# A fused attention and ternary-weight FFN block on eight cores: vector and scalar work of an attention tile spread otherwise over its four steps, weight scales in two steps, another order where the two phases meet

## The chip, the cores and the metric

The kernel runs on the 8 cores of one Trainium2 chip. Each core works on its own two sequences and no data passes between cores. The metric is the device time of the slowest core, in microseconds (us).

## The reference, cut to what matters

```python
x = L0_attn_x                      # (16, 2048, 1024) float32
x = x + attention(layernorm(x), w_qkv, w_out)   # 16 heads of 64, causal, window of 128 keys
x = x + ffn(layernorm(x), W1, b1, W2, b2)       # 1024 -> 4096 -> 1024
# attention: q, k, v = x @ w_qkv; softmax(q k^T / 8, masked) @ v; @ w_out
# ffn: h = gelu(bitlinear(x, W1, b1)); bitlinear(h, W2, b2)
def bitlinear(x, W, b):
    w_scale = clip(mean(abs(W)), 1e-5)           # one number for the whole matrix
    Wq = clip(round(W / w_scale), -1, 1) * w_scale
    x_scale = clip(max(abs(x), axis=-1), 1e-5)   # one number for each token
    xq = clip(round(x * 127 / x_scale), -128, 127) * x_scale / 127
    return xq @ Wq.T + b
```

## The kernel before, in words

A core has 32 tiles of 128 tokens. The program is written as lists of instructions for each engine (`QUEUE`), in the order in which the Python code calls the helpers; every engine runs its list in order and waits on semaphores (`tok`) for what it needs. So the place of a call in the code is the place in the queue of its engine, and for DMAs in the queue of SyncE (`sp`) or GpSimd (`pool`).

**Phase one** is attention. Its loop runs over 128 steps `j`, four (`c` = 0 to 3) for each tile `t`; step `c` treats four of the 16 heads. In step `j` TensorE gets: the scores of step `j + 1` (`s_pe`, tile `sc`), a first group of other matmuls (`f1`), the product of probabilities and values for step `j - 1` (`av_pe`, tile `av`), the transposes of the probabilities of step `j` (`t_pe`, tiles `tA`, `tB`), and a second group (`f2`). The groups come from `fill`: for c = 0 the queries and for c = 1 the keys of tile `t + 1` (`qk_pe`, 32 matmuls of 128 columns each), for c = 2 the output projection of tile `t - 1` (`o_pe`, 8 matmuls of 512 columns each), for c = 3 the values of tile `t + 1` (`v_pe`). Both groups go to the two banks `fb`, tile `f`. Their evictions (`e1`, and `e2`, which runs in the next step as `prev_ev`) are on ScalarE, but those of c = 2 are the residual adds on VectorE (`resid`, L238, `xr<-f,xr`); the second of them runs in step c = 3 and frees the bank for that step's `f2`.

In each step VectorE adds the mask to the four score tiles and takes their extremes (`ttr`, L455, `msc<-sc,masks`), ScalarE exponentiates (`ex`, `probs<-msc`), VectorE copies the transposed probabilities from PSUM (`pt_ev`, `PT<-tA`). `norm` divides by the sums (c = 2 for the first half of the heads, c = 0 of the next tile for the second), and `at_tr` transposes the result by DMA (`attnT<-attn`).

The layernorm ahead of attention goes by `ln1_stats` (VectorE, `lnc<-xr`), `ln1_rstd` (ScalarE), `ln1_nmr` (VectorE, one small operation, L339), `xln_` (GpSimd, `xln<-xr,lnc`) and `x_tr` (DMA transpose by SyncE, `xlnT<-xln`). Here the statistics of tile `t + 3` are in step c = 3, and the other four for tile `t + 2` at the end of step c = 0. The layernorm ahead of the FFN needs `ln2_sum` (mean, VectorE) and `ln2_sq` (sum of squares, ScalarE, `junk<-xr,nmean`); `spill` writes the tile to HBM by GpSimd's queue (`x1sp<-xr`). All three are at the end of step c = 0, two tiles later. `load_x` waits for the spill of the tile that had its buffer.

Besides, the FFN's weights are made ready in 128 **tasks**, one or two a step from step 4 on (`at_step`). `a1`, `a2` add up the absolute values of a piece of W1, W2 (even pieces on VectorE, odd ones on ScalarE); `q1`, `q2` quantize a piece: `task_pool` scales it on GpSimd one step ahead (`tern<-stg,wsc`), then VectorE clips it (`tern<-tern`) and writes fp8 (L668, `W1q<-tern`, `W2q<-tern`). Each piece is loaded by SyncE's queue (`task_load`, 512 KB, `stg<-w1t`, `stg<-w2t`). `scale_pe` makes the scale of a matrix: VectorE adds the sums, a matmul with ones adds over the partitions, VectorE divides.

**Phase two** is the FFN, a loop over 32 token tiles `it`: 8 groups of up projections of tile `it + 1` (`w1_pe`, banks `sc` and `f`), each evicted by `pre_gelu` (VectorE, `hb`), `gelu` (ScalarE), and `hmax`; then `fh`, `rnd` (ScalarE), `unoff` (VectorE) quantize, `tq` transposes by DMA (`hqT<-hq`), and `w2_pe` does the 64 down projections of tile `it` (`av<-W2q,hqT`). The input of a tile is read back by `load_x1`, `front_pool` subtracts the mean, `front_dve` takes the maximum and rounds, and `xt` transposes (`xlnT<-xln`). Where the phases meet, tiles 30 and 31 of phase one already carry `front_dve` for the first token tiles and up projections of token tile 0. The biases are loaded over the place of the qkv weights, once the last value matmul has read them.

Of the kernel before, what the change touches and what calls it, by code (L numbers as in the profile page):

```python
# [42 lines left out]
def _build(nt):  # L43
# [18 lines left out]
    def sb(name, n, dt, at=None):  # L62
# [3 lines left out]
        if at is None:  # L66
# [46 lines left out]
            for i in range(2, 6)]  # L113
    tern = [sb("tern%d" % i, D, BF16) for i in range(2)]
# [22 lines left out]
    yb = msc  # L137
    xqb = xln
    hqb = hq.bitcast(BF16)

    with ExitStack() as ctx:
# [452 lines left out]
        for i in range(32):  # L594
            tasks.append(("q1", i))
            tasks.append(("a2", i))
# [86 lines left out]

        def load_bias(i):
            if i < 4:
                tk["b1", i] = dma("sp", b1b[:, i * D:(i + 1) * D],
                                  b1_d[i * D:(i + 1) * D].partition_broadcast(
                                      128), d_bias[i], [tok("V", nt - 1, 1)])
            else:
                tk["b2"] = dma("sp", b2b, b2_d.partition_broadcast(128),  # L690
                               d_bias[4], [tok("V", nt - 1, 1)])

# [11 lines left out]
        def front_dve(t):  # L704
# [7 lines left out]
                   ALU.mult, ALU.mult, [r])  # L712
            tk["dq", t] = ts("dve", c[:, 4:5], c[:, 1:2], wsc[:, 3:4], None,
                             ALU.mult, waits=[a, tok("thr", 0)])
            a = ts("dve", xq, xcb[t % 2], c[:, 3:4], RND,
                   ALU.mult, ALU.add,
                   [r, tok("xqT", t - 1) if t else tok("xlnT", nt - 1)])
# [26 lines left out]
        def pre_gelu(t, u):  # L744
# [3 lines left out]
                hb[u % 4], ub[b], c[:, 4:5], b1b[:, u * 512:(u + 1) * 512],  # L748
# [106 lines left out]
        ln1_stats(2)  # L855
# [18 lines left out]
        assert max(j for j in range(nstep) if at_step[j]) <= nstep - 10  # L874
        to_load = list(range(ntask))
# [28 lines left out]
        for j in range(nstep):  # L904
# [14 lines left out]
            for n in mine:  # L919
                if n == 32:  # L920
                    scale_pe(0)
                if n == 96:
                    scale_pe(1)
                if n in (32, 96):
                    task_pool(n)
            for n in at_step[j + 1] if nxt else ():
                if tasks[n][0][0] == "q" and n not in (32, 96):
                    task_pool(n)
# [5 lines left out]
            if prev_ev is not None:  # L934
                prev_ev()
# [208 lines left out]
```

How the kernel before makes its waits and increments, by code:

```python
            def body(eng):  # L1079
                seen = {}
                for waits, fn, s, amt in QUEUE[q]:
                    for ws, val in waits:
                        if val > 0 and seen.get(ws.name, 0) < val:
                            eng.wait_ge(ws.h, val)
                            seen[ws.name] = val
                    if fn is None:
                        continue
                    ins = fn(eng)
                    if s is not None:
                        ins.then_inc(s.h, amt)
```

## Time and profile before

| | us |
|---|---|
| three runs: median (lowest to highest) | 1655.97 (1623.61 to 1711.35) |
| the profiled execution, its own time | 1623.96 |
| its span on the slowest core (core 6) | 1622.4 |
| the other cores' spans | 1607.0 to 1621.3 |
| TensorE busy (matmuls) | 1492.2 (92%) |
| VectorE busy | 1082.6 (67%) |
| ScalarE busy | 785.3 (48%) |
| GpSimd busy | 240.6 (15%) |
| mean granted TensorE clock | 0.985 |

The times are those of the slowest core in one execution. Busy time of an engine is the time in which it has an instruction at work; matmuls overlap, and are counted once. A stretch of the span in which no engine is full is one in which they wait for each other.

### The profile page before, as it was taken

What the parts mean: (1) busy time and instruction counts of PE and PEld (TensorE: products, weight loads), DVE (VectorE), ACT (ScalarE), POOL (GpSimd) and SP (SyncE); (2) the same over time, 40 slices, a digit from 0 to 9 for tenths busy, and PEclk for the clock granted to TensorE, in tenths of its full rate; (3) what the DMA queues carried; (4) which work ended last, traced back from release to release, by engine and by line L of the source; (5) the groups of instructions that cost most, each with busy time, mean ns of one, the idle gap of its engine ahead of it and who ended that gap; (6) DMA issues with size and microseconds to landing.
All of it is one profiled execution on the core that took longest, in us unless ns stands there. A gap on an engine that the chain in (4) does not pass through costs nothing.

```text
span 1622.4 us, 33796 instructions; the slowest of 8 cores (1607.0 to 1622.4 us)
## 1 busy us (share of the span) xinstructions
PE 1492.2 (92%) x11668; PEld 832.4 (51%) x11732; DVE 1082.6 (67%) x2704; ACT 785.3 (48%) x1826; POOL 240.6 (15%) x199
## 2 busy tenths in 40 slices
PE   2798799989999988977999999999999999999998
PEld 2566566666666666633444444444444444444443
DVE  2577788878888888666666666666666666666652
ACT  3677766766676666644433334233333333333331
POOL 0000022112212333102110101010101010110100
PEclk9899999999999999988999999999999999999999
DMA  9977767666655677352525343434435242435232
GB/s 299 266 194 215 210 176 221 190 196 196 212 155 170 180 173 174 84 130 59 111 66 110 66 103 74 97 79 82 94 73 104 66 107 63 111 66 111 65 85 53
DMA packets 277080, 214.25 MB, mean 132 GB/s; under 512 B 239280, under 2 KB 239408, under 8 KB 276912
## 3 DMA queue, kind: packets, MB, share of 16 engines
q1 hardware_dynamic: 272304, 195.31, 48.4%
q0 software_dynamic: 4608, 16.78, 3.0%
q8 instruction: 96, 1.57, 0.4%
q14 instruction: 72, 0.59, 0.1%
HBM read 120.29 MB, written 33.55 MB: 95 GB/s over the span
## 4 chain that ended last, share of the span: by engine, by line
PE 65%; DVE 14%; issue 6%; DMA 6%; ACT 5%; SPq 2%; POOL 1%; DVEq 0%; ACTq 0%; POOLq 0%
PE av L202 28%; PE f L202 23%; PE sc L202 14%; DVE msc L455 5%; DMA xr<-xc 2%; DVE PT L251 2%; ACT junk L218 2%; SPq L188 2%; DMA wst<-wqkv 1%; DVE absc L243 1%; DVE xr L238 1%; ACT probs L218 1%; DVE tern L225 1%; DMA x1sp<-xr 1%; DVE lnc L325 1%
## 5 line engine op out<-in xcount | busy, mean ns | idle before, releaser
L202 PE MATMUL av<-W2q,hqT 128*128 128x512 fp8e4 x2048 | 448.6, 380 | 3.4 <-DMA hqT<-hq 3.4
L218 ACT ACTIVATE hbuf<-hb 128x512 f32<-128x512 f32 x256 | 160.7, 629 | 460.6 <-DVE hb L235 460.5
L202 PEld LDWEIGHTS av<-W2q,hqT 128*128 128x128 bf16 x2048 | 200.9, 98 | 246.0 <-issue 5.7
L218 ACT ACTIVATE probs<-msc,cells 128x256 bf16<-128x256 f32 (+1 forms) x512 | 250.8, 491 | 145.6 <-DVE cells L455 111.9
L202 PE MATMUL f<-xlnT,wqkv_sb 128*128 128x128 bf16 x4096 | 254.6, 221 | 25.6 <-ACT qT L218 23.5
L202 PEld LDWEIGHTS f<-xlnT,wqkv_sb 128*128 128x128 bf16 x4096 | 235.5, 99 | 42.9 <-issue 42.4
L202 PE MATMUL f<-W1q,xlnT 128*128 128x512 fp8e4 x1040 | 238.0, 382 | 5.2 <-DVE hb L235 3.3
L202 PE MATMUL sc<-W1q,xlnT 128*128 128x512 fp8e4 x1008 | 230.2, 382 | 9.2 <-DVE hb L235 9.2
L455 DVE CUSTOM_DVE_ANT_0 msc<-sc,masks 128x256 f32<-128x256 f32 (+1 forms) x512 | 181.8, 410 | 26.5 <-PE sc L202 21.8
L218 ACT ACTIVATE hq<-hbuf,konst,fhc 128x1024 f16<-128x1024 f32 x128 | 148.3, 1229 | 93.4 <-DVE fhc L223 93.4
L202 PEld LDWEIGHTS f<-W1q,xlnT 128*128 128x128 bf16 x1040 | 101.9, 98 | 129.1 <-issue 8.7
L202 PEld LDWEIGHTS sc<-W1q,xlnT 128*128 128x128 bf16 x1008 | 98.9, 98 | 130.1 <-issue 12.8
L235 DVE SCALAR_TENSOR_TENSOR hb<-f,fqc,b1b 128x512 f32<-128x512 f32 x130 | 97.1, 748 | 89.9 <-PE f L202 87.9
L202 PE MATMUL f<-wqkv_sb,xlnT 128*128 128x512 bf16 x480 | 116.9, 386 | 38.9 <-ACT vh L218 17.7
L243 DVE TENSOR_REDUCE fhc<-hbuf 128x1 f32<-128x1024 f32 x128 | 152.0, 1208 | 0.0
L235 DVE SCALAR_TENSOR_TENSOR hb<-sc,fqc,b1b 128x512 f32<-128x512 f32 x126 | 94.2, 748 | 71.4 <-PE sc L202 71.1
L225 POOL TENSOR_SCALAR stg<-xr,nmean 128x1024 f32<-128x1024 f32 x32 | 35.9, 1121 | 697.2 <-DMA xr<-x1sp 552.0
L223 DVE TENSOR_SCALAR hq<-hq 128x1024 bf16<-128x1024 f16 x128 | 58.4, 458 | 110.2 <-ACT hq L218 110.2
L202 PE MATMUL f<-wout_sb,attnT 128*128 128x512 bf16 x465 | 111.0, 380 | 5.8 <-issue 4.9
L225 POOL TENSOR_SCALAR xln<-xr,lnc 128x1024 bf16<-128x1024 f32 x32 | 39.4, 1231 | 405.9 <-ACT qT L218 324.2
L218 ACT ACTIVATION_READ_ACCUMULATOR probs<-msc,cells 128x1 f32 x512 | 96.3, 188 | 0.0
L202 PEld LDWEIGHTS f<-wqkv_sb,xlnT 128*128 128x128 bf16 x512 | 45.8, 98 | 90.7 <-issue 46.0
(78 smaller groups left out, 1356.6 us busy)
## 6 DMA issues: line engine op xcount, KB each, us to landing
stg<-w1t SPq DMA_DIRECT2D x64, 512.0 KB, 7.8
stg<-w2t SPq DMA_DIRECT2D x64, 512.0 KB, 5.8
xr<-xc SPq DMA_DIRECT2D x32, 512.0 KB, 6.0
x1sp<-xr POOLq DMA_DIRECT2D x32, 512.0 KB, 3.4
xr<-x1sp SPq DMA_DIRECT2D x32, 512.0 KB, 5.4
y<-msc SPq DMA_DIRECT2D x32, 512.0 KB, 3.8
wst<-wqkv SPq DMA_DIRECT2D x24, 512.0 KB, 17.6
wst<-wout SPq DMA_DIRECT2D x8, 512.0 KB, 19.4
```

The source lines that it names most:

```text
L188: lambda e: e.dma_start(out=out, in_=in_), s, 16))
L202: return op("pe", lambda e: e.matmul(out=out, lhsT=lhsT, rhs=rhs, start=start, stop=stop), waits, sig)
L218: return op("act", lambda e: e.activation(out=out, in_=in_, func=func, **kw), waits)
L223: return op(q, lambda e: e.tensor_scalar(out=out, in0=in0, scalar1=s1, scalar2=None, op0=op0), waits)
L225: return op(q, lambda e: e.tensor_scalar(out=out, in0=in0, scalar1=s1, scalar2=s2, op0=op0, op1=op1), waits)
L235: return op("dve", lambda e: e.scalar_tensor_tensor(out=out, in0=in0, scalar=s, in1=in1, op0=op0, op1=op1), waits)
L238: return op("dve", lambda e: e.scalar_tensor_tensor(out=out, in0=in0, scalar=s, in1=in1, op0=op0, op1=op1, accum_out=accum), waits)
L243: return op("dve", lambda e: e.tensor_reduce(out=out, in_=in_, axis=AX.X, op=o, apply_absolute_value=absv), waits)
L251: return op("dve", lambda e: e.tensor_copy(out=out, in_=in_), waits)
L325: i=x[:, h * 512:(h + 1) * 512]: e.bn_stats(out=o, in_=i),
L455: e.tensor_tensor_reduce(out=u, in0=i, in1=m, scale=-0.125, scalar=BIG, op0=ALU.add, op1=ALU.min, accum_out=a), w)
```

## The change

The arithmetic is the same. In phase one, `ln1_stats` moves from c = 3 to c = 1, one tile later (for tile `t + 2`); `ln1_rstd` to c = 2, behind the first two exponentials; `ln1_nmr`, `xln_` and `x_tr` to c = 2, behind `norm`. `ln2_sum` and `spill` move to c = 3 of the tile in which the residual is added, and `ln2_sq` to c = 0 behind the first two exponentials. The copy of the probabilities goes to ScalarE at c = 2 when this step has a quantizing task (before: at c = 3, for the later tasks), and at c = 0 and 1 of the last tile.

The task list starts with four more sums of W2, so that quantizing begins later; `scale_pe` is split into `scale_sum`, one step after the last sum, and the matmul, one step after that.

Where the phases meet, the first 1024 biases get a buffer of their own, in the place of `tern`, and are loaded in tile 29 together with the first `load_x1`; `front_dve` is split into `front_max` and `front_q`, which move: those of token tile 0 to c = 1 and 2 of tile 30, those of tile 1 to c = 3 of tile 31, those of tile 2 into the loop of phase two. Four of the eight up projections of token tile 1 come between the last output projection and the loop.

```diff
+    b1q = sb("b1q", D, F32, at=tern_at)
...
         tasks = [("a1", i) for i in range(32)]
-        for i in range(32):
+        tasks += [("a2", i) for i in range(4)]
+        for i in range(28):
             tasks.append(("q1", i))
-            tasks.append(("a2", i))
+            tasks.append(("a2", i + 4))
+        tasks += [("q1", i) for i in range(28, 32)]
...
+        def scale_sum(g):
+            tk["wsum", g] = red(wsc[:, 10 + g:11 + g],
+                                absc[:, 32 * g:32 * g + 32],
+                                ALU.add, [tok("absa", g), tok("absv", g)])
+
         def scale_pe(g):
             b = tbank()
-            v = red(wsc[:, 10 + g:11 + g], absc[:, 32 * g:32 * g + 32],
-                    ALU.add, [tok("absa", g), tok("absv", g)])
             p = mm(tbf[b][:, 0:1], ones, wsc[:, 10 + g:11 + g], True, True,
-                   [v, tfree[b], tok("ones")], sig=True)
+                   [tok("wsum", g), tfree[b], tok("ones")], sig=True)
...
-        ln1_stats(2)
         for hh in range(4):
             ex(0, hh)
...
             if prev_ev is not None:
                 prev_ev()
+            if c == 3 and t >= 1:
+                ln2_sum(t - 1)
+                spill(t - 1)
             if nxt:
                 ex(j + 1, 0)
                 ex(j + 1, 1)
+            if c == 0 and t >= 2:
+                ln2_sq(t - 2)
+            if c == 2 and t + 2 < nt:
+                ln1_rstd(t + 2)
             if f1 is not None:
                 f1()
...
             if c == 2:
                 norm(t, 0)
+                if t + 2 < nt:
+                    ln1_nmr(t + 2)
+                    xln_(t + 2)
+                    x_tr(t + 2)
             t_pe(j)
-            pt_ev(j, on_act=(c == 3 and any(n >= 96 for n in mine)))
+            pt_ev(j, on_act=((c == 2 and any(tasks[n][0][0] == "q"
+                                             for n in mine))
+                             or (late and c < 2)))
...
-            if c == 0:
-                if t >= 2:
-                    ln2_sum(t - 2)
-                    ln2_sq(t - 2)
-                if t + 2 < nt:
-                    ln1_rstd(t + 2)
-                    ln1_nmr(t + 2)
-                    xln_(t + 2)
-                    x_tr(t + 2)
-                if t >= 2:
-                    spill(t - 2)
-            if c == 3 and t + 3 < nt:
-                ln1_stats(t + 3)
+            if c == 1 and t + 2 < nt:
+                ln1_stats(t + 2)
+            if j in sum_step:
+                scale_sum(sum_step[j])
+            if j - 1 in sum_step:
+                scale_pe(sum_step[j - 1])
...
+            if t == nt - 3 and c == 3:
+                load_x1(0)
+                load_bias(0)
             if t == nt - 2:
                 if c == 0:
-                    load_x1(0)
-                if c == 1:
                     ln2_rstd(0, nt - 4)
-                    load_x1(1)
                     front_pool(0, [tok("task", n) for n in
                                    range(ntask - 2, ntask)])
+                if c == 1:
+                    load_x1(1)
+                    front_max(0)
                 if c == 2:
-                    front_dve(0)
+                    front_q(0)
                     front_pool(1)
                 if c == 3:
                     xt(0)
-                    for i in range(5):
+                    for i in range(1, 5):
                         load_bias(i)
             if late:
-                if c == 0:
+                if c == 1:
                     load_x1(2)
-                    front_dve(1)
                 if c == 2:
                     for u in range(4):
                         gelu(0, u)
+                if c == 3:
+                    front_max(1)
+                    front_q(1)
...
-        for h in range(2):
-            o_pe(lt, h, av[:, h * 512:(h + 1) * 512], tok("N", lt, 1))
-            resid(lt, h, av[:, h * 512:(h + 1) * 512])
         hmax(0, 2)
         hmax(0, 3)
         fh(0)
+        for h in range(2):
+            o_pe(lt, h, av[:, h * 512:(h + 1) * 512], tok("N", lt, 1))
         for r in range(4):
             rnd(0, r)
-            unoff(0, r)
+        for u in range(4):
+            w1_pe(1, u)
+            pre_gelu(1, u)
+            unoff(0, u)
+        for r in range(4):
+            tq(0, r)
+        for u in range(4):
+            gelu(1, u)
...
-        front_dve(2)
...
+            if it == 0:
+                front_max(2)
+                front_q(2)
             if it + 2 < nt:
                 xt(it + 2)
```

## Rows read from the trace of the kernel before

**Rows 1.** Windows: length, then busy and (count) of PE, PEld, DVE, ACT, POOL; clock.

```profile
72.17:93.64 21.47, 18.34 (x236) 13.21 (x238) 15.15 (x51) 14.38 (x46) 1.20 (x1) 1.00 1.02 237
...
93.64:673.06 579.42, 520.36 (x6637) 372.66 (x6692) 469.29 (x1557) 399.47 (x1244) 121.23 (x121) 0.99 0.66 184
...
571.57:592.13 20.56, 18.60 (x240) 13.25 (x242) 17.13 (x57) 13.96 (x43) 6.20 (x6) 1.00 0.69 177
...
654.48:673.06 18.58, 18.27 (x239) 13.30 (x240) 11.86 (x48) 13.28 (x42) 2.24 (x3) 1.00 0.29 65
...
687.00:717.79 30.79, 22.15 (x143) 10.03 (x145) 19.92 (x65) 12.48 (x39) 0.70 (x2) 0.83 0.58 137
...
717.79:756.39 38.60, 27.56 (x136) 12.28 (x136) 27.99 (x47) 15.59 (x23) 12.62 (x8) 0.87 0.34 82
...
756.39:770.20 13.81, 13.81 (x65) 6.27 (x64) 8.47 (x19) 5.34 (x6) 0.00 (x0) 1.00 0.11 20
```

**Rows 2.** Timeline of TensorE in tile 25: start, length, instruction, idle before.

```profile
576.25 0.39 PE L202 MATMUL sc<-kT,qT 64*128 64x256 bf16 x4
...
581.26 0.39 PE L202 MATMUL sc<-kT,qT 64*128 64x256 bf16 x4
...
586.06 0.39 PE L202 MATMUL sc<-kT,qT 64*128 64x256 bf16 x4
...
590.52 1.67 PE L202 MATMUL f<-wqkv_sb,xlnT 128*128 128x512 bf16 x7 [1.56 <-ACT vh L218]
```

**Rows 3.** Timeline of the other engines in tile 25; one tile's instructions, ns.

```profile
578.86 0.16 DVE L339 SCALAR_TENSOR_TENSOR lnc<-lnc 128x1 f32<-128x1 f32 x1 [1.92 <-ACT lnc L218]
...
579.38 1.19 POOL L225 TENSOR_SCALAR xln<-xr,lnc 128x1024 bf16<-128x1024 f32 x1 [4.74 <-ACT qT L218]
...
580.71 1.93 SPq L197 DMA_TRANSPOSE xlnT<-xln  x1
...
580.96 1.86 DVE L668 TENSOR_SCALAR W2q<-tern 128x1024 fp8e4<-128x1024 bf16 x1
...
589.47 0.69 DVE L238 SCALAR_TENSOR_TENSOR xr<-f,xr 128x512 f32<-128x512 f32 x1
...
L668 DVE TENSOR_SCALAR W2q<-tern x32: 693/694/1864, 487.7 to 649.8; 128x1024 fp8e4<-128x1024 bf16 x32
```

**Rows 4.** Timeline, third step of tile 29, TensorE and VectorE.

```profile
663.85 0.39 PE L202 MATMUL sc<-kT,qT 64*128 64x256 bf16 x4
...
667.84 0.68 DVE L251 COPY PT<-tA 128x1024 bf16<-128x1024 bf16 x1
```

**Rows 5.** By tile, attnT and then xln, of 75:680: their transposing DMAs.

```profile
DMA to landing us min/median/max: 3.0/3.2/7.7
...
DMA to landing us min/median/max: 4.3/4.5/8.0
```

**Rows 6.** The start: timeline of SyncE; DMA issues of 71:72 and 76:77.5.

```profile
68.10 3.21 SPq L188 DMA_DIRECT2D stg<-w1t  x6
...
stg<-w1t SPq DMA_DIRECT2D x1, 512.0 KB, 13.0
...
attnT<-attn SPq DMA_TRANSPOSE x1, 7.7
```

**Rows 7.** Where the phases meet: DMA issue of 699:700; timeline of TensorE, VectorE.

```profile
attnT<-attn SPq DMA_TRANSPOSE x1, 11.5
...
708.92 3.57 PE L202 MATMUL f<-W1q,xlnT 128*128 128x512 fp8e4 x8 [3.34 <-DVE hb L235]
...
747.12 5.98 PE L202 MATMUL sc<-W1q,xlnT 128*128 128x512 fp8e4 x16 [9.18 <-DVE hb L235]
...
765.95 1.21 DVE L243 TENSOR_REDUCE fqc<-stg 128x1 f32<-128x1024 f32 x1
...
769.10 0.43 DVE L223 TENSOR_SCALAR xln<-xln 128x1024 bf16<-128x1024 f16 x1
```

More of the change, by code:

```diff
@@ L682, in load_x1 @@
                                 tok("sq", nt - 5 + t)] if t < 4 else []))
+        b1s = [b1q] + [b1b[:, i * D:(i + 1) * D] for i in range(1, 4)]
         def load_bias(i):
[L685 to L689, printed above, removed]
+            if i == 4:
                 tk["b2"] = dma("sp", b2b, b2_d.partition_broadcast(128),
                                d_bias[4], [tok("V", nt - 1, 1)])
+                return
+            w = [tok("V", nt - 1, 1)]
+            if i == 0:
+                w = [tok("ternq", 0), tok("ternq", 1)]
+            tk["b1", i] = dma("sp", b1s[i],
+                              b1_d[i * D:(i + 1) * D].partition_broadcast(128),
+                              d_bias[i], w)
         def front_pool(t, waits=()):
@@ L874, in _build @@
         assert max(j for j in range(nstep) if at_step[j]) <= nstep - 10
+        step_of = {n: j for j in range(nstep) for n in at_step[j]}
+        sum_step = {step_of[31] + 1: 0, step_of[91] + 1: 1}
         to_load = list(range(ntask))
@@ L918, in _build @@
                 task_load(to_load.pop(0))
[L919 to L925, printed above, removed]
             for n in at_step[j + 1] if nxt else ():
-                if tasks[n][0][0] == "q" and n not in (32, 96):
+                if tasks[n][0][0] == "q":
                     task_pool(n)
@@ L1031, in _build @@
         fh(0)
+        for h in range(2):
+            o_pe(lt, h, av[:, h * 512:(h + 1) * 512], tok("N", lt, 1))
         for r in range(4):
             rnd(0, r)
-            unoff(0, r)
+        for u in range(4):
[6 more added lines that the diff above has]
+            gelu(1, u)
+        for h in range(2):
+            resid(lt, h, av[:, h * 512:(h + 1) * 512])
+        ln2_sum(lt)
         for t in (lt - 1, lt):
-            ln2_sum(t)
             ln2_sq(t)
-            spill(t)
+        spill(lt)
         tk["out", -1] = tok("R", lt, 1)
@@ L1043, in _build @@
         add_bias(2)
-        front_dve(2)
         for it in range(nt):
-            for r in range(4):
-                tq(it, r)
             if it >= 1:
+                for r in range(4):
+                    tq(it, r)
                 out(it - 1)
@@ L1055, in _build @@
                 for u in range(8):
-                    w1_pe(it + 1, u)
-                    pre_gelu(it + 1, u)
-                    gelu(it + 1, u)
+                    if it >= 1 or u >= 4:
+                        w1_pe(it + 1, u)
+                        pre_gelu(it + 1, u)
+                        gelu(it + 1, u)
                     if u % 2 == 1 and u >= 3:
@@ L1072, in _build @@
                     add_bias(it + 3)
-                    front_dve(it + 3)
+                    front_max(it + 3)
+                    front_q(it + 3)
             w2_pe(it, 0, 32)
```

10 lines of the change are left out of this document (7 added, 3 removed).

## The prediction

> **What bounds the kernel now.** I read the chain of waits first. From 770 us on it is nothing but matmuls, 27.6 us for each of the token tiles, so the second phase is bound by TensorE and no edit there that only moves other engines' work can gain. That leaves the 756 us before it. I therefore cut the first phase at the first score matmul of each tile, by windows [rows 1]. Tiles 2 to 29 take 579.42 us, 20.69 on average. Tile 29, which carries no weight pieces, takes 18.58: its four steps are 4.68, 4.68, 4.56 and 4.66, and they are matmuls back to back. So 18.5 is TensorE's own floor for a tile, and some 2.1 us a tile are waits. The reader is to see in a tile that carries pieces (tile 25, 20.56) where they lie: its steps begin at 571.57, 576.25, 581.26, 586.06 and the next tile at 592.13, thus 4.68, 5.01, 4.80 and 6.07 [rows 1, 2]. The fourth step waits before its second group of value matmuls, which start 4.46 us into the step [rows 2]; the groups ahead of it take 2.75 when nothing waits. The profile names ScalarE there, but that had finished; the bank is freed by the residual add on VectorE, which began only at 589.47 [rows 3].
>
> Why VectorE is late is seen one step earlier. In the first step it stands idle 1.92 us for the small norm scale of ScalarE, which itself waited for the mean [rows 3]; in the second its write of a quantized piece takes 1.86 instead of 0.69, while GpSimd works beside it [rows 3]. VectorE is 17.13 of 20.56 us busy in this tile [rows 1], so nothing gives that time back.
>
> The meeting of the phases costs more: 30.79 us from 687.00 (last step of tile 30) to 717.79, with 22.15 busy on TensorE, and 38.60 from there to the first down projection at 756.39, with 27.56 busy [rows 1]. Stalls of 3.34 and 9.18 us stand in it (and one of 3 us at its start), and after them the matmuls run for some 6 us at the lower of the two clock levels, 1.2 instead of 2.4 GHz: 16 matmuls take 5.98 [rows 7] instead of the 3.45 that 13.81 for 64 gives [rows 1]; the granted clock of both windows is 0.83 and 0.87 [rows 1].
>
> **The change, part by part.** Steps are counted 1 to 4 (c = 0 to 3), times in a step from its score matmuls.
>
> (1) Statistics and rescaling leave the fourth and first step. The mean goes to step 4 and the square sum to the middle of step 1, both of work that was ready long before; statistics go to step 2, the rest of the norm to step 3. The instructions stay the same in number. What goes is the idle time of 1.92 us; with it the query eviction is no longer behind the square sum, so steps 1 and 2 go to 4.68 each: 0.33 in tile 25, more where it is 6 to 7 us today. Statistics in step 2 put some 1.6 us where the idle time and the collision used to be; VectorE then reaches step 3 at 0.55, just on time.
>
> (2) The normalised input is now made in step 3, after the first half of the attention normalisation. Tile 29 shows a step 3 that VectorE entered on time: matmuls at 663.85, probability copy at 667.84, so the small scale comes at 4.0 [rows 4]. GpSimd starts 0.52 after it (578.86 to 579.38), takes 1.19, and the transposing DMA is issued 0.14 later [rows 3]: at 5.85. It used to have some 15 us before it was needed; now TensorE asks for it at 9.45 (two steps and 0.33). That leaves 3.6 us. Its price is the landing: 3.2 us is the median of the attention transposes, 4.5 that of the input's, 8.0 the worst [rows 5]. I take 3.2, since the input's present place is beside the spill and task loads, and the new one is like that of the attention's. At 3.2 the wait is nothing; at 4.5 it is 0.9 in tiles without another delay.
>
> (3) GpSimd's 1.19 us now lie from 4.5 to 5.7 in step 3, right where VectorE quantizes if step 3 has such a piece. Its write starts at 4.65 and is held as in tile 25, by the 1.05 us left of GpSimd's operation, to 6.3. Four score operations (1.38) put the residual add at 7.65, and TensorE's group 1.05 after its start (589.47 to 590.52 [rows 2, 3]), at 8.7. Today that is 590.52 - 581.26 = 9.26 [rows 2]. Steps 3 and 4 together: from 10.87 to 10.3; tile 4.68 x 2 + 10.3 = 19.7. That the probability copy is on ScalarE in this step is what makes it no worse. 15 of the 28 tiles are of this kind (from the task list). 7 have an absolute sum of VectorE (1.2 us) in step 3, which lies before the residual add and moves the rest by 0.8: 19.2. In 6 neither: 18.8, with 0.3 over the floor for the residual add in step 4. Sum 15 x 19.7 + 7 x 19.2 + 6 x 18.8 = 543; 3 for three tiles with two pieces in step 2, 3 for the full queues up to tile 5, and 0.2 a tile, 5.6, for small waits that no row gives. 554 against 579.4: **-25** (bounds -36 with none of these additions, +33 with every landing at 6.2, see B).
>
> The Trainium skill (SBUF — State Buffer, Who interferes with whom) says that a VectorE operation in its two-port modes and a GpSimd operation hold one port pair by turns, each for the whole instruction. The trace agrees for VectorE, 1.86 against 0.69. By the page the transfer could also be late, if VectorE's 0.42 us operation is first; without any such rule the 15 tiles would be 18.8 and the sum 13 lower.
>
> (4) The weight scales in two steps. At tile 6 TensorE stood before the ones-matmul for VectorE, which waited for a load held back by the spill, ahead of the sum; with spill and statistics moved, and sum and matmul one step apart, it goes. It is in the 28 tiles already. The new order of tasks changes no count: nothing.
>
> (5) **The start.** The input of tile 2 was transposed in the first step of tile 0. Now it is queued in step 3, behind the first six weight loads on SyncE's queue. These are issued from 68.10 for 3.21 us and the last takes 13.0 us to land, to 84 [rows 6]. An attention transpose issued at 76.84 took 7.7 us, to 84.5 [rows 6], so the queue serves in order. The new transpose is issued at 71.4 and lands at 84, while TensorE wants it 0.33 after 72.17 [rows 1]: 12 us of wait, and 2 for the clock behind it as above. Tile 1 takes 21.47 now [rows 1] against 19.2 for its kind in (3); what it waits more, behind the same loads, falls into the new wait, -2. **+12**; bounds +3 (landing after 4.5 us) and +15.
>
> The Trainium skill (DMA: Bandwidth & Descriptors, Queues, rings and completion order) says that each DMA engine consumes the descriptors of a ring in order. The attention transpose agrees. Were it not so here, the start would cost 3 and the sum 9 less.
>
> (6) Tiles 30 and 31. The front of the second phase (3.65 us of VectorE, 765.95 to 769.53 [rows 7]) is split: maximum in step 2 of tile 30, rounding in step 3. VectorE then enters step 4 about 1 us late instead of 3.3: step 4 takes 5.9. The first bias is loaded early into another buffer, and the front of token tile 1 leaves this stretch; steps 1 to 3 of tile 31 could be 4.56. But four bias loads of 512 KB still stand before the attention transpose on the same queue. It took 11.5 us to land behind five [rows 7]; I take 9.3 behind four, from 3.3: it lands at 12.6 where step 3 wants it at 9.45, 3.2 us, and 1 for the clock. 5.9 + 3 x 4.56 + 4.2 = 23.8 against 30.79: **-7** (-3 to -11).
>
> (7) Tail. The maximum and rounding of token tile 1 (3.6 us) now lie before the evictions and the last normalisation, so the last attention transpose lands at 13.2 and TensorE, out of work at 7.8, waits 5.5 us there (it was 1.9). Then it has no 9.18 us stall: four of the eight up projections of tile 1 fill the time of rounding. Sum: 4.1 (step 4) + 0.2 + 3.45 + 5.5 + 3.45 + 13.8 = 30.5, and 2.5 for the clock, 33.0 against 38.60: **-5.5** (-2 to -8).
>
> (8) In the first round of the second phase the front of token tile 2 now comes only after the rounding of tile 1. Today's front at that place ends at 769.53, 13.1 after the down projection began [rows 7]; a transpose of 3.0 to 3.2 lands at 772.7, and TensorE wants it at 770.20 [rows 1]: **+3** (2.5 to 6, with the clock).
>
> Sum: -25 + 12 - 7 - 5.5 + 3 = -22.5, against the 1623.96 of the profiled execution (span 1622.4): 1601. Of the three runs the lowest, 1623.61, is like it; the median is 1655.97, 2% above, and I forecast for executions like the profiled one. Some 2% is what a measurement of this kernel can tell from no change.
>
> **Rivals.** (B) **The transposed input is late in every tile.** The place is the first query matmul of each tile; the room is 3.6 us in 13 tiles and 4.6 in the 15 with a collision. For it speaks the 8.0 and the loads of 512 KB that share the queue; against it the 3.2. It decides from a landing of 5.0 us: 15 x 0.4 + 13 x 1.4 = 24 eats the whole gain, 1625. At 5.5 it is 15 x 0.9 + 13 x 1.9 = 38: 1639, slower than before; at 6.2 it is 1659.
> (C) **Less is lost at the joints.** The start costs 3 or its wait swallows more of tiles 1 and 2 (-9), and the small waits of (3) don't come (-6): 1586. For it: tile 29 at 18.58.
> (D) **VectorE is the new bound.** It has some 16 us of work a tile; with gaps at each hand-over tiles stay at 20.2, and the gain in (3) is 28 x 0.49 = 14 instead of 25: 1612. For it: 83% busy already [rows 1]; against it: the idle 1.92 that goes.
>
> **Numbers.** My forecast 0.48, B 0.13, C 0.22, D 0.17. Predicted 1600. The range of 8 in 10 runs from 1582, below C, to 1636, near B at 5.5; it leaves out a third of C and half of B. Faster by over 2% is below 1591.5: C and 0.08 of the forecast, 0.3. Slower by over 2% is B at 6.2: 0.05. Within 2%: 0.65.
>
> **What would show it.** Tile windows of 18.8 to 19.7; no idle VectorE before the small scale; the write of a piece at 1.6 to 1.8 us in step 3 and 0.69 in step 2; TensorE idle from 72 to 84 for a transposed input; 5 us idle before the last output projection; one stall of some 3 us after the first down projection. Wrong would make it above all another landing time of the input's transposes, or weight loads that finish earlier at the start.

## The result and the profile after

| | before | after |
|---|---|---|
| median of four runs each (lowest to highest), us | 1641.91 (1623.61 to 1711.35) | 1599.43 (1596.05 to 1616.81) |
| the profiled execution, us | 1623.96 | 1599.56 |
| spans of the cores, us | 1607.0 to 1622.4 | 1582.0 to 1597.7 |
| ratio after / before, 95% | | 0.9833 (0.9804 to 0.9861) |

The change makes the kernel 1.7% faster; 1600 was predicted (the sum of its terms gives 1601.5). In some executions the chip grants the cores a lower clock for a long time (up to 1759 us for the kernel before); the ratios here are of executions without that.

The head of the page of after (core 5, the slowest) shows no other amount of work, only less waiting: TensorE 1503.5 us of 1597.7.

```profile
span 1597.7 us, 33901 instructions; the slowest of 8 cores (1582.0 to 1597.7 us)
...
PE 1503.5 (94%) x11732; PEld 839.8 (53%) x11732; DVE 1071.5 (67%) x2695; ACT 797.2 (50%) x1835; POOL 248.2 (16%) x199
```

The windows of after answer to [rows 1]; columns as there. They are tile 1, tiles 2 to 29, from the last step of tile 30 to that of tile 31, from there to the first down projection, and from that to the next up projection.

```profile
74.26:104.64 30.38, 21.37 (x237) 15.98 (x238) 16.07 (x53) 14.11 (x44) 1.92 (x2) 0.83 0.56 125
104.64:654.40 549.76, 525.63 (x6694) 375.51 (x6694) 462.33 (x1551) 410.13 (x1251) 128.93 (x120) 0.99 0.73 196
668.32:694.59 26.27, 21.40 (x145) 10.34 (x145) 14.44 (x51) 15.79 (x43) 0.58 (x1) 0.87 0.59 141
694.59:726.17 31.58, 26.82 (x137) 12.15 (x136) 23.08 (x46) 13.09 (x18) 4.31 (x4) 0.95 0.39 91
726.17:743.42 17.25, 13.98 (x66) 6.17 (x65) 12.85 (x26) 5.90 (x6) 8.33 (x5) 1.00 0.19 44
```

So against [rows 1] tile 1 loses 8.91 us (and begins 2.09 later), the 28 tiles gain 29.66, the meeting of the phases 4.52 and 7.02, and the first round of the second phase loses 3.44, with 1.7 more in the up projections behind it (15.5 for 13.8, at the lower clock). Together 25, and the spans differ by 24.7.

**The start.** DMA issue of 71 to 72, then the timeline of TensorE:

```profile
xlnT<-xln SPq DMA_TRANSPOSE x1, 11.9
```
```profile
83.47 3.57 PE L204 MATMUL f<-xlnT,wqkv_sb 128*128 128x128 bf16 x32 [8.81 <-DMA xlnT<-xln]
...
90.80 1.96 PE L204 MATMUL f<-xlnT,wqkv_sb 128*128 128x128 bf16 x32
```

The input of tile 2, transposed behind the six weight loads, lands after 11.9 us, and TensorE stands 8.81 for it. Behind the wait the same 32 matmuls take 3.57, later 1.96: the lower of the two clock levels.

**A tile.** First the sums by tile over 100 to 640 or 650 us. Before (core 6), what the small scale waited for, and how often:

```profile
  ACT lnc L218: 52.6, 27
```

After (core 5) no such line is left. The rows are the write of a piece and GpSimd's rescaling (ns: least, median, most), then what TensorE waited for the input's transposes, and their landing:

```profile
L675 DVE TENSOR_SCALAR W2q<-tern x32: 693/694/1425, 480.5 to 631.2; 128x1024 fp8e4<-128x1024 bf16 x32
...
L227 POOL TENSOR_SCALAR xln<-xr,lnc x29: 1180/1551/1695, 100.4 to 649.8; 128x1024 bf16<-128x1024 f32 x29
...
  PE f L204: 5.0, 9
DMA to landing us min/median/max: 3.0/3.1/5.1
```

The 52.6 us in 27 waits are gone. The transposes land after 3.1, and TensorE waited for them 5.0 us in 28 tiles. The timeline of VectorE and GpSimd in the third step of a tile with a piece to quantize:

```profile
552.60 0.15 DVE L341 SCALAR_TENSOR_TENSOR lnc<-lnc 128x1 f32<-128x1 f32 x1
552.67 0.42 DVE L227 TENSOR_SCALAR tern<-tern 128x1024 bf16<-128x1024 bf16 x1
...
553.19 0.69 DVE L675 TENSOR_SCALAR W2q<-tern 128x1024 fp8e4<-128x1024 bf16 x1
553.40 1.55 POOL L227 TENSOR_SCALAR xln<-xr,lnc 128x1024 bf16<-128x1024 f32 x1 [3.66 <-DVE tern L227]
```

Here the collision of the prediction happens, the other way round: VectorE's write takes its 0.69, and GpSimd's operation 1.55 instead of 1.19. Of the 64 such writes on this core four are still held, up to 1.43 us; before it was 15, up to 1.86.

**The joints.** TensorE's three stalls that are left:

```profile
687.60 3.57 PE L204 MATMUL f<-wout_sb,attnT 128*128 128x512 bf16 x8 [3.97 <-DMA attnT<-attn]
...
707.33 5.19 PE L204 MATMUL av<-wout_sb,attnT 128*128 128x512 bf16 x16 [4.76 <-DVE fhc L245]
...
743.42 1.93 PE L204 MATMUL sc<-W1q,xlnT 128*128 128x512 fp8e4 x7 [3.27 <-DMA xlnT<-xln]
```

The attention transpose behind the bias loads, the last attention tile behind the front of token tile 1, and the input of token tile 2: the three that the prediction named.

### The profile page after: what moved, and what is told of

Same layout as the page of the kernel before. It is cut to its first block, busy times and chain, and to the rows that moved or that the text cites. A ratio compares the mean times of both kernels' runs of the same rounds, so it can differ in the third digit from the quotient of the medians.

```text
span 1597.7 us, 33901 instructions; the slowest of 8 cores (1582.0 to 1597.7 us)
## 1 busy us (share of the span) xinstructions
PE 1503.5 (94%) x11732; PEld 839.8 (53%) x11732; DVE 1071.5 (67%) x2695; ACT 797.2 (50%) x1835; POOL 248.2 (16%) x199
## 4 chain that ended last, share of the span: by engine, by line
PE 75%; DVE 10%; DMA 5%; issue 5%; ACT 2%; SPq 2%; POOL 1%; DVEq 0%; ACTq 0%; POOLq 0%
PE f L204 30%; PE av L204 28%; PE sc L204 15%; DVE msc L457 3%; DMA xlnT<-xln 2%; SPq L190 2%; DMA attnT<-attn 2%; DMA wst<-wqkv 1%; ACT probs L220 1%; DVE xr L240 1%; DVE lnc L327 1%; DVE tern L227 1%; PE tB L209 1%; PE tA L209 1%; DVE PT L253 1%
## 5 line engine op out<-in xcount | busy, mean ns | idle before, releaser
L204 PE MATMUL f<-xlnT,wqkv_sb 128*128 128x128 bf16 x4096 | 259.0, 223 | 25.3 <-DMA xlnT<-xln 13.8
L204 PEld LDWEIGHTS f<-xlnT,wqkv_sb 128*128 128x128 bf16 x4096 | 241.0, 100 | 39.6 <-issue 39.1
L220 ACT ACTIVATE hq<-hbuf,konst,fhc 128x1024 f16<-128x1024 f32 x128 | 148.4, 1229 | 92.3 <-DVE fhc L225 85.5
L204 PE MATMUL f<-wqkv_sb,xlnT 128*128 128x512 bf16 x512 | 124.2, 387 | 16.9 <-ACT wqkv_sb L220 8.6
L204 PE MATMUL f<-wout_sb,attnT 128*128 128x512 bf16 x496 | 119.7, 385 | 7.0 <-DMA attnT<-attn 7.0
L227 POOL TENSOR_SCALAR xln<-xr,lnc 128x1024 bf16<-128x1024 f32 x32 | 46.2, 1444 | 372.7 <-DVE lnc L341 169.7
L227 POOL TENSOR_SCALAR tern<-stg,wsc 128x1024 bf16<-128x1024 f32 x64 | 72.3, 1130 | 114.9 <-DMA stg<-w2t 36.9
L204 PEld LDWEIGHTS f<-wqkv_sb,xlnT 128*128 128x128 bf16 x512 | 46.0, 99 | 74.6 <-issue 29.7
```

The lines of the kernel that those rows point to most:

```text
L204: return op("pe", lambda e: e.matmul(out=out, lhsT=lhsT, rhs=rhs, start=start, stop=stop), waits, sig)
L220: return op("act", lambda e: e.activation(out=out, in_=in_, func=func, **kw), waits)
L227: return op(q, lambda e: e.tensor_scalar(out=out, in0=in0, scalar1=s1, scalar2=s2, op0=op0, op1=op1), waits)
```

## The experiments

All are edits of the changed kernel. The table has, for each, the median over its eight cores of the time between the same first matmuls: to tile 1, tile 1, tiles 2 to 29, the two stretches where the phases meet, the first down projection with what follows it, and the up projections behind it. Most rows are a single execution. How well the columns repeat is seen in e2, e7, e9, e10 and e11, which are the same kernel up to the last step of tile 30: 544.1 to 545.3 in tiles 2 to 29, but 92.3 to 96.6 in start and tile 1 together.

| us | start | tile 1 | 2 to 29 | joint | tail | down | up |
|---|---|---|---|---|---|---|---|
| before | 71.8 | 22.6 | 575.8 | 29.2 | 38.4 | 13.8 | 13.8 |
| after | 73.8 | 30.3 | 545.7 | 23.1 | 32.4 | 17.2 | 15.1 |
| e1_loads_later | 72.6 | 25.8 | 543.0 | 23.8 | 31.4 | 17.2 | 15.5 |
| e2_ln1_back | 71.4 | 21.1 | 544.2 | 21.1 | 31.8 | 16.9 | 13.8 |
| e3_ln2_back | 73.0 | 29.6 | 541.4 | 23.5 | 31.4 | 17.9 | 15.5 |
| e4_load_ahead | 72.8 | 28.9 | 556.1 | 23.6 | 32.0 | 17.2 | 16.1 |
| e5b_both_back | 71.6 | 22.2 | 562.8 | 22.0 | 32.1 | 17.0 | 15.3 |
| e6_copy_back | 71.6 | 20.8 | 550.2 | 22.5 | 31.9 | 17.0 | 14.5 |
| e7_best | 71.3 | 22.1 | 544.1 | 19.4 | 26.9 | 13.8 | 22.2 |
| e9_pool_first | 71.3 | 21.0 | 545.3 | 19.4 | 26.9 | 13.8 | 22.6 |
| e10_front2_in_loop | 71.5 | 20.9 | 545.2 | 19.4 | 26.9 | 17.5 | 15.3 |
| e11_bias_after_write | 72.3 | 24.3 | 544.6 | 19.4 | 26.9 | 13.8 | 13.8 |
| e12_scale_at_once | 72.7 | 24.0 | 550.0 | 21.9 | 32.7 | 16.8 | 15.2 |

**e1_loads_later**: is it the six loads that the transpose of tile 2 waits for?

```diff
-            while j >= 2 and to_load and (...):
+            while j >= 3 and to_load and (...):
                 task_load(to_load.pop(0))
```

> The changed kernel with one edit: the first weight loads are put on SyncE's queue one step later (from step 3 of the loop on, not 2), so that the transpose of tile 2's input stands ahead of the first six. Theory (the queue serves in order): TensorE's wait of 11.5 us in the first step of tile 1 shrinks to 1 to 3 us, since the transpose lands some 3 to 4 us after its issue near 70; the loads come 3 us later and cost nothing; tile 2 begins near 95 instead of 104.6; time 1599.6 - 9 = 1590. Rival (the memory is busy with all cores' loads at this time, whatever the order): the transpose still takes 8 us or more, or the next tiles wait for the loads, and tile 2 begins at 100 or later; 1596 to 1600.

Measured 1599.09. The DMA issues of 69 to 72 on core 4:

```profile
xlnT<-xln SPq DMA_TRANSPOSE x1, 3.5
```

3.5 instead of 11.9, so the loads ahead were the cause; the first step of tile 1 falls from some 16 us to some 5. But tile 1 gives back only 4.5 of the 9, since its second and third steps now take some 7 and 9 us, with the same loads in the queue (in after 4.7 and 4.6). The theory of 1590 missed: the wait goes, but half of it comes back in the next two steps. The total says nothing more, since its slowest core took 557.2 in tiles 2 to 29, where the median is 543.0.

**e2_ln1_back**: the layernorm-1 chain in its old steps, all else as changed.

```diff
+        ln1_stats(2)                       # ahead of the steps
-            if c == 2 and t + 2 < nt:  ln1_rstd(t + 2)
-                if t + 2 < nt:             # c == 2, after norm(t, 0)
-                    ln1_nmr(t + 2); xln_(t + 2); x_tr(t + 2)
-            if c == 1 and t + 2 < nt:  ln1_stats(t + 2)
+            if c == 0 and t + 2 < nt:
+                ln1_rstd(t + 2); ln1_nmr(t + 2); xln_(t + 2); x_tr(t + 2)
+            if c == 3 and t + 3 < nt:  ln1_stats(t + 3)
```

> The changed kernel with the layernorm ahead of attention where it was before (statistics at c = 3, the small scale, GpSimd's scaling and the transpose at the end of c = 0), everything else as changed; the transposed input has its 15 us of room again, and the start is as before. Theory (the gain in the tiles needs both: VectorE no longer idle for the small scale, and GpSimd's operation away from the quantizing write of step 2): VectorE idles 0.6 to 0.9 us a tile instead of 1.92, writes of 1.86 are back at c = 1, step 4 is long again; tiles 2 to 29 take 562 to 568 instead of 549.8; the start gives 10 back; time 1599.6 + 15 - 10 = 1603 to 1607. Rival (the early mean alone is what freed the tiles): tiles 2 to 29 stay near 550 and the time is 1589.

1582.04, against 1626.7 for the kernel before on that chip. Start and tile 1 together fall by 11.6, and the tiles don't get longer (544.2). The theory (562 to 568) missed, and its rival, that the early mean alone freed the tiles, was right. So the moved chain costs all of the start and, beside the early mean, earns nothing. The small scale waits again, half as long as before (by tile, core 5), 1.07 each, which the step absorbs:

```profile
  ACT lnc L220: 29.9, 28
```

**e3_ln2_back**: the other move undone alone.

```diff
-            if c == 3 and t >= 1:  ln2_sum(t - 1); spill(t - 1)
-            if c == 0 and t >= 2:  ln2_sq(t - 2)         # mid-step
+            if c == 0 and t >= 2:
+                ln2_sum(t - 2); ln2_sq(t - 2); spill(t - 2)   # end of step
```

> The changed kernel with mean, sum of squares and spill where they were before (end of c = 0, two tiles later), everything else as changed. Theory: nobody on VectorE waits for the square sum any more, so only the query eviction on ScalarE behind it is late, 0.3 us a tile, and loads of x wait for the spill with four steps of room: tiles 2 to 29 take 555 to 560, time 1605 to 1610. Rival (the late spill, which holds SyncE's queue, was the cost): tiles of the first third 1 us or more longer, 565 and above, time 1615.

1593.97, tiles 541.4, where the theory had 555 to 560. So beside the moved chain the early mean earns nothing either.

The two runs together also speak against the collision as the cost. In e2, 14 to 19 of the 64 writes of pieces on each core are held, most for 1.42 us, in e3 one or two, and the tiles differ by 2.8 us.

**e5_both_back, e5b_both_back**: both moves undone; copy of the probabilities and scales as changed.

> The changed kernel with both moves undone, the layernorm ahead of attention and the mean, square sum and spill all at their places of before, while the copy of the probabilities on ScalarE at c = 2, the new task order, the split scale and the joints stay as changed. Undone alone, either move left tiles 2 to 29 at 541 to 544 us (median of the cores), as short as the 545.7 of the changed kernel; before they were 575.8. Theory (the chain mean, square sum, small scale at the end of c = 0 is what cost, and either move breaks it): with both undone the chain is back, VectorE idles 1.92 us a tile for the small scale, and tiles 2 to 29 take 562 to 570; what is left to 575.8 is the scale's stall and the copy. Rival (neither move gives anything; the gain is that of the copy and the task order): tiles 2 to 29 at 541 to 548, time 1582 to 1588.

> The changed kernel with both moves in the tiles undone (layernorm-1 chain in step 0 and its moments in step 3; mean, squares and spill of layernorm 2 in step 0), the copy of the probabilities left in step 2. Theory: either move alone breaks the chain of mean, squares, moments and small scale at the end of step 0, and only with both undone it comes back: VectorE's idle time ahead of the small scale is 50 us in all, tiles 2 to 29 take 565 to 572 us, the whole 1603 to 1610 us. Rival: the copy of the probabilities or the split scale earned the gain, then the tiles stay at 545 to 550 us and the whole at 1582 to 1590 us.

In the first (1705.37) the mean granted clock was 0.91 to 0.93; only cores 0 and 1 had 1.00 in the first phase, and their tiles 2 to 29 take 570.3 and 561.6 us. The second, the same kernel, 1606.51, has 562.8 in the tiles, and VectorE's wait for the small scale is the old one, 2.0 us each (by tile, core 4):

```profile
  ACT lnc L220: 54.2, 27
```

So mean, square sum and small scale in one step end form a chain; **either move cuts it, and the cut is worth 562.8 - 544.2 = 18.6 us**, with copy and scales as changed. The time of the rerun lies in the theory's range, its tiles are 2 below.

**e6_copy_back**: e2 with the copy of the probabilities on ScalarE in the fourth step, as before, not in the third.

```diff
-            pt_ev(j, on_act=((c == 2 and any(tasks[n][0][0] == "q" for n in mine))
+            pt_ev(j, on_act=((c == 3 and any(n >= 96 for n in mine))
                              or (late and c < 2)))
```

> The run with the layernorm ahead of attention put back (1582.04), and besides the copy of the probabilities on ScalarE at c = 3 for the late tasks, as before, instead of c = 2. Theory (VectorE's work in c = 2, then the mask and the residual add of c = 3, is what TensorE waits for in the fourth step): c = 3 grows by 0.5 to 0.6 us in the tiles with a quantizing piece in c = 2, tiles 2 to 29 take 8 to 12 us more, 552 to 556 (median of the cores). Rival (the copy's place doesn't matter, since it only moves 0.6 us from one step to the next on an engine that catches up): 544 to 547.

1589.39, tiles 550.2: the copy's place is worth 6.0 us, less than the theory's 8 to 12 and more than the rival's nothing.

**e12_scale_at_once**: e2 with sum and matrix product of a weight scale in one step.

```diff
-            if j - 1 in sum_step:
-                scale_pe(sum_step[j - 1])
+            if j in sum_step:
+                scale_pe(sum_step[j])
```

> The kernel with the layernorm-1 chain back, with the sum for a weight scale and its matrix product in one step again. Theory: it happens twice in the run and nobody waits for it within a step, so the tiles stay at 544 to 547 us and the whole at 1580 to 1584 us. Rival: the split scale is the part of the gain that the chain (18 us) and the copy of the probabilities (6 us) leave open; then the tiles take 549 to 552 us and the whole 1587 to 1590 us.

1597.47 (the profiled execution) and 1592.47, ratio 0.9806, tiles 550.0: the theory missed, by time and by tiles, and the rival's tiles are right. The loss stands in the two places, tile 7 (21.6 for 19.1) and tiles 19 and 20 (20.9 and 20.3 for 18.6 and 19.3). The timeline of core 4, VectorE and TensorE:

```profile
202.43 0.18 DVE L245 TENSOR_REDUCE wsc<-absc 128x1 f32<-128x32 f32 x1
```
```profile
202.87 0.35 PE L204 MATMUL tB<-wsc,ones 128*128 128x1 f32 x2 [4.01 <-DVE wsc L245]
```

Two small matmuls, 0.35 us together, stand at the head of TensorE's list for 4.01 us, since VectorE comes to the small sum only at the end of the step. The kernel before has the same wait (TensorE from 100 to 650 us, core 6: total, times, longest):

```profile
PE tA L202 <- DVE wsc L243: 5.6, 2, 5.3
```

The split is worth 5.8 us in the tiles. Another 4.2 us of this kernel's loss lie in the start and tile 1, which are as long in e11 without this edit, and some 3 in the joint and behind it, which this edit doesn't touch.

The account of the 28 tiles closes with it: 544.2 + 18.6 + 6.0 + 5.8 = 574.6, against 575.8 before. It adds up three differences that were each measured alone; the new order of the tasks was not undone in any run.

**e4_load_ahead**: is the room of 3.6 us in (2) real, and does a load just ahead hold the transpose back? The load of the input of tile t+3 moves from the second step to right before the transpose.

```diff
-            if c == 1 and 2 <= t and t + 3 < nt:
-                load_x(t + 3)
...
                     xln_(t + 2)
+                    load_x(t + 3)     # SyncE waits for the rescaling first
                     x_tr(t + 2)
```

> The changed kernel with the 512 KB load of a later tile's x put right ahead of the transpose of the input on SyncE's queue in c = 2 (it was at c = 1), in 27 tiles. It measures the room of 3.6 us that the prediction gave the transpose. Theory (rooms as worked out, queue in order): the transpose lands some 5.5 to 6.5 us after its issue instead of 3.1, TensorE waits 2 to 2.5 us for it in the first step of nearly every tile, tiles 2 to 29 take 590 to 610 and the time is 1640 to 1660. Rival (the transpose has more room than 3.6 us, or does not queue behind the load): the wait is under 0.5 us a tile and the time within 10 us of 1600.

1613.55, tiles 556.1, ten more; the theory's 590 to 610 missed by far. By tile, core 4: what TensorE waited for the transposes, and their landing:

```profile
  PE f L204: 12.1, 16
DMA to landing us min/median/max: 3.0/3.8/6.2
```

On this core 16 transposes took over 3.6 us, and TensorE waited for each of them; on all eight cores it was 99 of 101. So the room was right. What the theory had wrong is how long a load holds a transpose. The DMA issues of 377 to 380:

```profile
xr<-xc SPq DMA_DIRECT2D x1, 512.0 KB, 3.3
xlnT<-xln SPq DMA_TRANSPOSE x1, 4.7
```

The load is issued 1.5 us ahead (at 377.63 and 379.17) and lands first, at 380.9, the transpose at 383.9. So it is in all 216 pairs of the eight cores: the load is issued 1.5 to 2.2 us ahead and has landed 1.9 us (median) after the transpose's issue, within the 3.1 that a transpose takes alone, and no transpose lands before it.

**e7_best**: e2 and three repairs: bias loads 2 to 4 behind the attention transpose of tile 30, the front of token tile 1 behind the last normalisation, that of token tile 2 ahead of the loop of the second phase.

```diff
                 if c == 3:
                     xt(0)
-                    for i in range(1, 5):
-                        load_bias(i)
+                    load_bias(1)          # 2 to 4 go behind at_tr(30)
-                if c == 3:                # tile 31
-                    front_max(1); front_q(1)
         norm(lt, 1)
         at_tr(lt)
+        front_max(1); front_q(1)
...
         add_bias(2)
+        front_max(2); front_q(2)
         for it in range(nt):
-            if it == 0:  front_max(2); front_q(2)
```

> The run with the layernorm ahead of attention put back, and three edits where the phases meet: bias loads 2 to 4 behind the attention transpose of tile 30 (they were ahead); the front of token tile 1 behind the last attention normalisation (it was ahead); the front of token tile 2 ahead of the loop of phase two (it was in its first round). Theory (each of the three stalls has the named cause): step 3 of tile 31 loses its wait of 3 to 4 us and the slow clock behind it (joint 21 to 18.5); TensorE's wait before the last output projection goes from 5 to 2 us (tail 31.8 to 27.5); the wait after the first down projection goes (16.9 to 13.8). Together 1582 - 10 = 1572. Rival (VectorE's same work only comes elsewhere): the front of tile 1 holds the evictions of up projections and the front of tile 2 the first rounding, so the tail stays at 31 or more and the time is 1577 to 1582.

1579.46, ratio to before 0.9738 (0.9706 to 0.9769): the three stalls have the named causes, but the time is the rival's. The joint falls to 19.4, the tail to 26.9, the stall in the first round goes; but 22.2 us of up projections follow instead of 13.8. VectorE waits 6.41 us for the input of token tile 2, which GpSimd prepares behind two bias additions:

```profile
700.16 1.22 DVE L245 TENSOR_REDUCE fqc<-stg 128x1 f32<-128x1024 f32 x1 [6.41 <-POOL stg L227]
```

**e9_pool_first** and **e10_front2_in_loop**: e7 with that operation of GpSimd issued first; and e7 without the third repair.

```diff
+        front_pool(2)                     # e9: ahead of the last tile's spill
         for h in range(2):
             resid(lt, h, av[:, h * 512:(h + 1) * 512])
...
         add_bias(0)
         add_bias(1)
-        front_pool(2)
```

> As the kernel with all joints mended (layernorm-1 chain back in its old steps, bias loads 2 to 4 behind attnT of tile 30, the front of token tile 1 behind the last norm, that of token tile 2 ahead of phase two's loop), but with GpSimd's xcb of token tile 2 issued ahead of the last tile's spill and of the two bias additions of 2.3 us each. Theory: the 6.4 us for which VectorE stood at 699 to 706 us were a wait for GpSimd's place in its own order; without it the up projections behind the first down projection fall from 22.2 us to 15, and the time from 1577 us (lowest of that kernel) to 1569 to 1572, a ratio to before of 0.965 to 0.968. Rival: VectorE is late there by its own work (the front of token tile 2 is 3 to 4 us of it), then the stretch stays at 20 us or more and the ratio at 0.972 to 0.975.

> Layernorm-1 chain back, bias loads 2 to 4 behind attnT of tile 30, front of token tile 1 behind the last norm, but the front of token tile 2 where the changed kernel has it, in the first round of phase two. Theory of a sum: 1582 less 1.7 (joint) less 4.9 (tail) = 1575 us, a ratio of 0.969 to 0.972, with a stall of 3 to 3.6 us left before the first down projection. Rival: freeing the last projection earlier only moves the wait to the first round of phase two, and the time stays at 1580 to 1583 us (ratio 0.973 to 0.976).

e9: 0.9740 (0.9717 to 0.9763), the stretch still 22.6: the theory missed, and the numbers are the rival's, though not for its reason. VectorE no longer waits, but on core 4 its timeline and GpSimd's show

```profile
705.01 6.97 DVE L227 TENSOR_SCALAR xln<-stg,fqc 128x1024 f16<-128x1024 f32 x1
712.08 2.37 DVE L225 TENSOR_SCALAR xln<-xln 128x1024 bf16<-128x1024 f16 x1
...
730.29 0.75 DVE L227 TENSOR_SCALAR xln<-stg,fqc 128x1024 f16<-128x1024 f32 x1
731.15 0.43 DVE L225 TENSOR_SCALAR xln<-xln 128x1024 bf16<-128x1024 f16 x1
```
```profile
703.37 6.95 POOL L232 TENSOR_TENSOR xr<-xr,b2b 128x1024 f32<-128x1024 f32 x3
710.31 1.11 POOL L227 TENSOR_SCALAR stg<-xr,nmean 128x1024 f32<-128x1024 f32 x1
711.57 2.60 POOL L232 TENSOR_TENSOR xr<-xr,b2b 128x1024 f32<-128x1024 f32 x1
```

Two writes that take 0.75 and 0.43 alone take 6.97 and 2.37 beside GpSimd's additions, and TensorE stalls 6.66 us after them. e10, where VectorE does this front from 709.25, after GpSimd's additions, has 0.9715 (0.9688 to 0.9741), as its theory of a sum had it.

**e11_bias_after_write**: e9, with the additions waiting for those writes.

```diff
-        add_bias(0)
+        front_max(2); front_q(2)
+        add_bias(0, [tok("xq", 2)])
         add_bias(1)
         add_bias(2)
-        front_max(2); front_q(2)
```

> As the kernel before it (all joints mended, GpSimd's xcb of token tile 2 ahead of the spill), but GpSimd's three bias additions wait for VectorE's second write of the front of token tile 2. Theory: there VectorE's two writes took 6.97 and 2.37 us instead of 0.75 and 0.43 because GpSimd's three additions (703.37 to 710.32, and 711.57 to 714.17) ran beside them; with the additions behind, they take 0.75 and 0.43, the rounding of token tile 1 comes 8 us earlier, TensorE's stall of 6.66 us goes, the stretch behind the first down projection falls from 22.6 to 14 to 15.5 us, and the ratio to before to 0.967 to 0.970. Rival: the writes are slow for another reason (their source or target), then they stay at several us, the stretch at 20 us or more and the ratio at 0.973 to 0.976.

Median 1575.26, ratio 0.9683 (0.9656 to 0.9711), the best here. The stretches from the joint on are 19.4, 26.9, 13.8 and 13.8. VectorE and GpSimd on core 4:

```profile
703.57 0.76 DVE L227 TENSOR_SCALAR xln<-stg,fqc 128x1024 f16<-128x1024 f32 x1
704.43 0.43 DVE L225 TENSOR_SCALAR xln<-xln 128x1024 bf16<-128x1024 f16 x1
```
```profile
705.01 6.98 POOL L232 TENSOR_TENSOR xr<-xr,b2b 128x1024 f32<-128x1024 f32 x3 [3.11 <-DVE xln L225]
```

The same work one after the other: 8.15 us less on VectorE for 3.11 us in which GpSimd waits and nobody waits for it.

## Why the prediction was right, and where it was not

The total was right, 1600 for 1599.4, and so was each large term. By its numbers:

(1) and (3), the tiles: 549.8 for 554, a gain of 29.7 for 25. The idle time before the small scale went as said. Two things in their reading were wrong. The first is the cause: I put the gain to both moves together, and e2, e3 and e5b show that either alone cuts the chain; the layernorm-1 chain was moved at a price of 11 us and earns nothing beside the other.

The second is who is held in the collision: VectorE's write was to take 1.6 to 1.8 in step 3, and it took 0.69, while GpSimd's operation went from 1.19 to 1.55. VectorE's short operation of 0.42 was first, and its write too (553.19, GpSimd's at 553.40). By the Trainium skill (SBUF — State Buffer, Who interferes with whom) whichever of the two is issued first has the shared ports for its whole instruction and the other blocks; the trace agrees, and it is the case that (3) named behind its sum and left out of it. The 0.4 us fall on a transfer that has room, not on VectorE.

The 4.7 by which the gain was put too low are not there, though. On core 5 the 15 tiles with a piece to quantize in step 3 took 296.1, as forecast (15 x 19.7 = 295.5). The last nine of them, 18.9 to 19.7 each, are below it, and tiles 10, 17 and 18, with 20.9, 21.2 and 22.3, above, so that the agreement is in part chance. The seven with a sum took 140.2 for 134.4, the other six 113.5 for 112.8; all 28 are 7 us over the sum without additions, where the prediction had added 11.6. It is these additions that were too large. And e2 beside e3, with many held writes and with almost none, leaves at most some 3 us for them, which speaks against the collision as the reason for 19.7.

(2) The input in the third step: room of 3.6, landing 3.2 taken, 3.1 measured; TensorE waited 5.0 us in all. Rival B is ruled out. e4 confirms the room.

(3), the copy of the probabilities on ScalarE: called what makes it no worse; measured 6.0 us (e6).

(4) Scales: called a thing in the tiles, without a number. It is 5.8 us (e12), and my expectation for e12 that nobody waits was wrong although the prediction had described that very wait.

(5) The start: +12 forecast (84 less 72.5 is 11.5, rounded up); 2.1 + 8.9 = 11.0 measured. The 8.9 come by the mechanism named: landing after 11.9 for the 12.6 taken (84 less 71.4). The 2.1 by which tile 1 begins later are in no term; they go with the moved chain (start 71.4 in e2, 73.0 in e3): ahead of the scores of tile 0's last step TensorE waits 1.8 us for VectorE (0.8 before and in e2), and the 8 matmuls behind take 3.47 instead of 1.89, at the lower clock level. e1 adds that issuing the loads one step later gives back only some half of it. That the queue serves in order holds: in the traces of before, after, e1 and e4 no transfer on SyncE's queue lands before the one issued ahead of it.

(6) -4.5 for -7: the step is the attention transpose behind the bias loads. 3.2 us of wait were forecast, 3.97 came, and the low clock behind it cost 8 matmuls 3.57 instead of 1.89, then 2.51 for the next: 2.3 us, not 1. The two cores compared have the longest of these stretches (25.6 to 30.8 before, 20.0 to 26.3 after); by the medians of the table it is -6.1.

(7) -7.0 for -5.5: the idle 5.5 before the last output projection was 4.76; the low clock cost 5.19 - 3.61 = 1.6, not 2.5.

(8) +3 forecast, 3.4 and 1.7 for the clock measured, inside the bounds.

Rival C (1586) had two halves: that the start costs 3, where it cost 11, and that the small waits of (3) don't come, -6, where the tiles were 4.7 lower. Rival D (tiles of 20.2) is ruled out by 19.6. That the total agrees so closely is in part luck: the terms were off by -4.7, -1, +2.5, -1.5 and +2.1, which leaves -2.6, and the forecast of 1600 stood 1.5 below its own sum.

## What to carry to other kernels

When a change breaks a chain in two places, run each half alone: here either half alone earned all that both did, and one of them cost 11 us at the start. An instruction on an in-order engine whose input comes late in a step belongs one step later, however short it is. And before an operation is moved to where an engine is free, look at what the engine beside it does with the same memory: one wait between GpSimd's additions and VectorE's writes took TensorE's stretch from 22.6 us to 13.8.

## What was not expected of the hardware

GpSimd's operations in a row can hold VectorE's write for longer than one of them. In e9 the write was issued at 705.01, when the first of three additions (2.3 us each) had run 1.64 us; it ended at 711.98, after the third had ended at 710.32 and the next operation (1.11) at 711.42. On all eight cores it took 6.95 to 6.98. GpSimd paused for 0.15 us between 711.42 and 711.57, and no row shows VectorE's write getting on before that. By the Trainium skill (SBUF — State Buffer, Who interferes with whom) whoever issues first has the shared ports for its whole instruction; here VectorE's write did not get them when that instruction ended, and waited for the next ones too. In e11 a maximum of 1.21 us and two bias additions from PSUM of 0.70 each, on VectorE, ran beside GpSimd's additions and were not longer than elsewhere, so not every operation is held.

A transposing DMA behind one load of 512 KB landed after 3.8 us in the median (e4, core 4), behind six after 11.9, alone 3.1. Both fit a queue that lands in the order of issue. In e4 the one load had landed some 1.9 us after the transpose's issue. In the start of after (core 5) the six loads, issued from 67.83 to 70.16, land one after another from 71.92 to 82.32, and the transpose 0.9 us behind the last. What holds a transpose is thus not that a load stands ahead of it, but when the last one ahead of it lands. How much the other cores' loads slow these six was not measured.
